# Two attention layers and two routed FFNs on one core: the bodies of the first FFN ahead of those of the second

## The reference

```python
x = x + attention0(layernorm(x), ctx, ctx)        # 32 query heads, 8 key heads of 8, no mask
x = x + ffn0(layernorm(x))                        # 2 experts, the better one per row
x = x + attention1(layernorm(x), ctx, Wq, Wkv, Wout)   # 16 heads of 16, causal
x = x + ffn1(layernorm(x))                        # 8 experts, two per row, and a shared one

# ffn0: h = n @ w_fc[e].T (256 -> 1024); a = square(where(h >= 0, h, h / 2)); a @ w_proj[e].T
# ffn1: h = n @ down_w + down_b (256 -> 128)
#       for the two experts of a row: gelu(gelu(h) @ w1 + b1) @ w2 + b2, by its gate
#       (the other experts get h = 0, whose result is the same for each row)
#       + 0.1 * the shared expert;  @ up_w + up_b;  + gelu(n) @ core_w + core_b
```

## Time and profile before

| | |
|---|---|
| median of 3 runs | 417.0 us (416.74 to 418.52) |
| the profiled execution | 420.97 us |
| its span, first to last instruction | 419.2 us |
| TensorE busy | 89% of the span |
| vector, scalar, GpSimd busy | 56%, 53%, 22% |
| mean granted TensorE clock | 0.935 of 2.4 GHz |
| DMA | busy in the first 3 of 40 slices |

### The profile page before, as it was taken

One profiled execution on the slowest core, in us unless ns is written; L12 is line 12 of the kernel. 1 busy time (PEld: TensorE's weight loads), 2 busy tenths in 40 slices (PEclk: granted clock), 3 DMA queues, 4 the chain that ended last, 5 costly groups with the idle time before them and its releaser, 6 DMA issues.

```text
span 419.2 us, 9361 instructions
## 1 busy us (share of the span) xinstructions
PE 373.0 (89%) x3768; PEld 302.9 (72%) x3768; DVE 235.2 (56%) x611; ACT 221.3 (53%) x419; POOL 93.3 (22%) x173
## 2 busy tenths in 40 slices
PE   3355939999999999997999999899998999996896
PEld 1343838888888877987778888588876888775574
DVE  4798494869587447788344212855348036436242
ACT  2344832654654555595684312667644236775662
POOL 7872112322123032310001334000053120002000
PEclk9975776999999999997999999699999999999699
DMA  9990000000000000000000000000000000000000
GB/s 190 410 396 11 2 0 2 2 2 2 2 2 0 3 2 2 2 2 0 2 3 27 2 0 1 2 1 2 14 16 1 2 0 2 3 2 25 0 2 26
DMA packets 8218, 12.16 MB, mean 29 GB/s; under 512 B 4464, under 2 KB 6768, under 8 KB 7408
## 3 DMA queue, kind: packets, MB, share of 16 engines
q1 hardware_dynamic: 8176, 11.57, 8.3%
HBM read 10.52 MB, written 1.05 MB: 28 GB/s over the span
## 4 chain that ended last, share of the span: by engine, by line
PE 73%; DVE 16%; ACT 5%; issue 3%; POOL 2%; POOLq 0%; DVEq 0%; ACTq 0%
PE Y L1226 23%; PE H L1226 22%; PE S L1226 15%; PE S L1267 4%; PE S L1327 3%; PE S L1291 1%; PE S L1234 1%; DVE PT L990 1%; DVE MN L989 1%; ACT A L778 1%; PE S L1243 1%; PE S L1392 1%; ACT L778 1%; DVE K L976 1%; DVE KT L1057 1%
## 5 line engine op out<-in xcount | busy, mean ns | idle before, releaser
L1226 PE MATMUL H<-XT,WF 128*128 128x256 f32 x256 | 62.5, 395 | 0.0
L869 POOL TENSOR_TENSOR A<-R 128x512 f32<-128x512 f32 x32 | 33.3, 1039 | 125.8 <-PE Y L1226 74.9
L1226 PE MATMUL Y<-WP,A 128*128 128x256 f32 x256 | 59.5, 382 | 0.0
L1226 PE MATMUL H<-GH,W 128*128 128x256 f32 x168 | 50.6, 407 | 7.1 <-ACT GH L769 4.2
L778 ACT ACTIVATE A<-H,B 128x256 f32<-128x256 f32 x84 | 38.9, 475 | 32.1 <-PE Y L1226 22.7
L1226 PEld LDWEIGHTS H<-XT,WF 128*128 128x128 f32 x256 | 49.0, 198 | 8.4 <-ACT R L752 0.8
L1226 PEld LDWEIGHTS Y<-WP,A 128*128 128x128 f32 x256 | 47.3, 190 | 6.1
L1226 PE MATMUL Y<-A,W 128*128 128x256 f32 x168 | 50.5, 397 | 0.2 <-ACT A L778 0.2
L752 ACT ACTIVATE R<-H 128x512 f32<-128x512 f32 x32 | 19.1, 597 | 46.2 <-PE H L1226 46.1
L1226 PEld LDWEIGHTS H<-GH,W 128*128 128x128 f32 x168 | 30.7, 199 | 14.4 <-ACT A L778 5.9
L1180 DVE TENSOR_TENSOR YG<-YS,Y 128x256 f32<-128x256 f32 x32 | 13.4, 420 | 39.1 <-ACT YS L795 39.0
(11 more groups left out here) (183 smaller groups left out, 647.1 us busy)
## 6 DMA issues: line engine op xcount, KB each, us to landing
W<-in_w SPq DMA_DIRECT2D x2, 1344.0 KB, 11.0
WF<-in_wf SPq DMA_DIRECT2D x2, 1024.0 KB, 7.8
WP<-in_wp SPq DMA_DIRECT2D x2, 1024.0 KB, 9.8
X<-in_x SPq DMA_DIRECT2D x8, 128.0 KB, 8.4
out_dram<-X SPq DMA_DIRECT2D x8, 128.0 KB, 1.7
CD<-in_ctx_in SPq DMA_DIRECT2D x2, 256.0 KB, 5.4
C<-in_ctx_in SPq DMA_DIRECT2D x1, 256.0 KB, 2.9
CT<-in_ctxT SPq DMA_DIRECT2D x1, 256.0 KB, 3.9
```

Of the source, the lines that this page charges most:

```text
L869: nc.gpsimd.tensor_tensor(flat(A0[:, n % 2, :, :]), R0[:, n % 2, :], R0[:, n % 2, :], ALU.mult).then_inc(a0_ready, 1)
L1226: return nc.tensor.matmul(o, a, b, start=start, stop=stop, skip_group_check=shared)
```

## The change

The order of bodies becomes all four of `ffn0`, then all four of `ffn1`. The numbers by which the planner weighs urgency, table loads, array changes and slack are others. Because the turned rows of one `ffn1` group may now be copied to XT1 soon after the GELU that reads those of the group before, this copy has a function of its own with a wait for that GELU (`gx_ready`).

```diff
-SWITCH = 5.3
-CHANGE = 8.0
-SLACK = {"pe": 0.039, "act": 0.052, "dve": 0.154, "pool": 0.024}
+SWITCH = 3.6
+CHANGE = 0.9
+SLACK = {"pe": 0.04, "act": 0.18, "dve": 0.31, "pool": 0.0}
...
-           "ffn0": (-33.7, 4.9), "ffn0_body": (-114.2, -4.5), "ffn1": (669.6, -114.4), "ffn1_body": (-36.9, 30.7),
+           "ffn0": (29.6, -29.4), "ffn0_body": (-151.7, -36.0), "ffn1": (617.6, -203.4),
...
-BODIES = [("ffn0", 0)] + [x for g in range(GROUPS - 1) for x in (("ffn0", g + 1), ("ffn1", g))] + [("ffn1", GROUPS - 1)]
+BODIES = [("ffn0", g) for g in range(GROUPS)] + [("ffn1", g) for g in range(GROUPS)]
...
-            h |= evacuate("ffn1", "x", lambda g, i: flat(XT1[:, :, :]), lambda b, i: b[:, :])
...
+            def turned_rows1(g, _):
+                b, done = filled(act, "ffn1", g, "x", 0)
+                if g:
+
+                    act.wait_ge(gx_ready, g)
+                nc.scalar.copy(flat(XT1[:, :, :]), b[:, :]).then_inc(done, 1)
```

More of the change, by code:

```diff
@@ L91 @@
 BODY = {("ffn0", "u"), ("ffn0", "d"), ("ffn0", "y"), ("ffn1", "c"), ("ffn1", "w"), ("ffn1", "y"), ("ffn1", "o")}
-URGENCY = {"attn0": (38.7, 20.0), "attn1": (-9.9, 32.6), "attn1_keys": (-23.0, -18.9),
-           "ffn0": (-33.7, 4.9), "ffn0_body": (-114.2, -4.5), "ffn1": (669.6, -114.4), "ffn1_body": (-36.9, 30.7),
-           "zero": (-347.7, 19.6), "constg": (-587.6, 61.3), "constm": (64.6, -29.8), "consti": (-58.3, 210.5)}
-BODIES = [("ffn0", 0)] + [x for g in range(GROUPS - 1) for x in (("ffn0", g + 1), ("ffn1", g))] + [("ffn1", GROUPS - 1)]
+URGENCY = {"attn0": (-3.3, -7.3), "attn1": (-12.5, 37.0), "attn1_keys": (-24.8, -58.7),
+           "ffn0": (29.6, -29.4), "ffn0_body": (-151.7, -36.0), "ffn1": (617.6, -203.4),
+           "ffn1_body": (-38.2, 30.7), "zero": (-524.0, 1.4), "constg": (-652.0, -20.7),
+           "constm": (-58.8, 97.7), "consti": (-191.2, 169.6)}
+BODIES = [("ffn0", g) for g in range(GROUPS)] + [("ffn1", g) for g in range(GROUPS)]
 def work_of(s):
@@ L799, in _ @@
                      ("ffn0", "g"): exps("ffn0", E0), ("ffn0", "u"): leaky, ("ffn1", "e"): exps("ffn1", E1),
-                     ("ffn1", "t"): top_exp, ("ffn1", "b"): gelu_biases, ("ffn1", "d"): inner,
+                     ("ffn1", "t"): top_exp, ("ffn1", "b"): gelu_biases, ("ffn1", "d"): inner, ("ffn1", "x"): turned_rows1,
                      ("ffn1", "c"): hidden, ("ffn1", "y"): expert})
```

## The result

The changed kernel takes 405.5 us, the median of 4 runs (402.2 to 407.1), against 417.1 before: ratio 0.9705, 95% interval 0.9636 to 0.9774. On another chip, with 6 runs, the ratio was 0.9728 (0.9698 to 0.9759). The forecast was 406.6. Its profiled execution took 407.12, span 405.2.

The account below looks back on a forecast made before the run. TensorE, busy 89% of the span, bounds the kernel; winnable time lies in the start and five stretches (20.6 us). Terms -5.0 - 4.3 - 3.7 - 1.2 - 1.4 - 1.3 + 4.5 + 2.0 = -10.4 from 417.0 give 406.6, range 399 to 418.

Parts of the forecast that it names:

- The start, -5: Before the first FFN's first up-projection: XN near 54.5, first H at 60 to 61 us, 5 us earlier; bounds 0 and -8.
- Group 0: Second FFN's first group: zero rows no longer among query turns; 0.5 of 4.8 us left, term -4.3.
- the border of bodies 0 to 1: Second FFN, group 1: 1.0 of 4.7 us left, term -3.7; sign: under 1.5 us idle.
- the border of bodies 1 to 2: Second FFN, group 2: gates ready early, two table loads; 1.0 of 2.2 us left, term -1.2; sign: under 1.5 idle.
- End of the attention: Stretch 368-382 us before, now under bodies 1 and 2: 0.8 of 2.2 us left, term -1.4.
- Last group: Second FFN, group 3: two table loads, not four, one gap of 3.1 us; 5.4 of 6.7 left, term -1.3.
- New places to wait, +2: From 60 to 230 us, attention fills the first FFN's bodies in an untraced order: +2 us, bounds 0 and 6.
- Array changes, +4.5: TensorE changes between tiled and whole array, 83 to 111, 0.16 us each: +4.5; sign: busy minus idle about 4 us longer.
- Table loads: Scalar engine: sixteen table loads, a switch costing 1.28 us; with the skill page's drain 2.66, result near 409.4.
- The added wait, 0: Copy of turned rows for groups 1 to 3 waits for the previous group's GELU: 0, at most 0.1 us a group.
- The slower one: Rival: second FFN bodies in a row each pay 8.9 us at their border; +19.3, 425.9 us; chance 0.13.
- The one in which the clock holds: Rival: no clock fall in the last lead-in (2.3) and no new waits (2.0); -14.7, 402.3 us; chance 0.15.

Follow-up runs that it names:

- old start, changed order behind: Changed kernel with every engine's list up to the first FFN's second down-projection as in the kernel before; 410.7 us, ratio 0.9815.
- changed, again: The changed kernel run again, unchanged, in a second series on another chip; 407.2 us, ratio 0.9728.
- late gates: Changed kernel with the last group's gates' turn behind two hidden chunks on TensorE, its copy behind the first hidden GELU; 404.3 us, ratio 0.9678.
- three moves: Changed kernel with the gates' turns of groups 0 and 3 and the turn of tile 6's attention result moved later; 401.8 us, ratio 0.9625.
- The moves: Changed kernel with five steps later on TensorE: gates' turns (groups 0, 3), query turns (tiles 6, 7), attention result's turn (tile 6); 406.1 us, ratio 0.9708.
- the three parts made alone: Kernel before with only the new start, 417.5 us, or only new SWITCH, CHANGE and SLACK, 439.1; changed kernel with all old planner numbers, 431.7.

## Why the prediction was right, and where it was not

The sum was right to 1.1 us (-11.6 measured, -10.4 forecast). Most of its steps stand, but that it came so close is in part luck. Between the two profiles, from which the terms were counted, the difference is 13.85; the profile of before was 4.0 above its median, that of the changed kernel 1.6. And terms that were too small and too large cancel.

*The start, -5.* H at 60.81, within the 60 to 61, and XN at 55.57, 1 us behind the 54.5. By my own formula the term is larger, 34.9 - 27.1 = 7.8 in the two profiles, and of another kind. I took H's earlier place as the gain and the half clock only as a bound (-8). In the first 80 us, TensorE's idle time fell by little and the clock's cost by much:

| first 80 us | idle | clock |
|---|---|---|
| before | 28.9 | 13.2 |
| old start, changed order behind | 29.1 | 11.5 |
| changed | 27.1 | 6.5 |
| changed, again | 28.1 | 7.1 |
| late gates | 27.8 | 8.6 |
| three moves | 27.6 | 5.6 |

So the start gives 1 to 2 us of idle time and 3 to 8 of clock. The reason given, that what now stands behind H is hidden because TensorE is never empty from there, is true only of the changed order: with the old one the same start gained nothing.

*Groups of the second FFN.* Group 0: no wait on its zero rows and none from 240 to 264 us. But its gates' turn waits 1.20 at 236, which I had not priced, and in five of seven traces with this wait a half clock follows (1.6 in this one). So 2.8 instead of 0.5 in this trace. Left at the border of bodies 0 to 1: 2.7 us instead of 1.0, three waits for keys and queries of tiles 6 and 7 (0.68, 0.79, 1.24), not for GX. This fails the sign "under 1.5 us idle". That term was too small because I counted the TensorE time of these steps, 6 us, as cover, and not that their turns wait for vector and GpSimd work. The moves also showed that those of the queries can't simply be put off. At the border of bodies 1 to 2: 0.9, as forecast. End of the attention: 0.3 instead of 0.8. Last group: 3.25 idle in one gap and 1.3 of clock, 4.5 instead of 5.4.

*New places to wait, +2.* In the stretch that I named, 60 to 230 us, TensorE is idle for only 0.4, at clock 1.00: the term was too large. What no term held is a half clock at 274 us, 1.7, with no gap ahead of it (see the last section).

*Array changes, +4.5.* 0.163 measured by itself, for one pair of shapes, against 0.16 read from two rows: 28 of them would be 4.6. In the kernel the work at full clock rose by only 2.4, in the second trace by 1.6; the sign "about 4 us longer" did not come. So the price holds for the change itself, and whether all 28 are paid in full in the kernel stays open.

*Table loads.* Sixteen. A switch costs 1.28 again: the load at 373.28 ends at 374.56, GX starts at 374.58. By the Trainium skill, "ScalarE: Activation LUTs", "What ACT_TABLE_LOAD costs", a drain of 1.38 would stand in between; it is not seen in this trace either.

*The added wait, 0*, as seen above.

With measured sizes, in the profiles: -7.8 for the start, 13.7 - 20.6 = -6.9 behind 80 us, +4.6: -10.1 against -13.85. The split of the span says where the 3.8 are. Idle and clock fell by 16.4, 1.7 more than these stretches hold: 1.0 of it is small waits of the kernel before outside my five stretches, the rest clock ahead of 59 us. And work at full clock rose by 2.4, 2.2 less than the changes would cost; that part stays open.

*The rivals.* The slower one (four bodies in a row each pay at their border) is not this kernel's case, but it was near: the same order of bodies under the old numbers takes 431.7, above its 425.9. I had priced the finished order and not the numbers that led to it; that was sound for this kernel, and says nothing of its neighbours. The one in which the clock holds, 402.3, is met in its number by the fastest run, which has the highest mean clock of the four. No trace of that run shows where it held:

| changed kernel, run | us | mean granted clock |
|---|---|---|
| fastest | 402.19 | 0.974 |
| | 404.49 | 0.966 |
| | 406.46 | 0.962 |
| profiled | 407.12 | 0.962 |

## What to carry to other kernels

Price a new plan from its finished order, stretch by stretch, and not part by part: here the three parts made alone cost 0, 15 and 22 us and all together gained 11.6. An earlier start of the bottleneck's main work gained nothing here where the steps behind it were not ready, and its worth is read from idle time and clock, not from where its first row stands. Once a plan is made, look for steps that its engine waits for and move them by hand behind one block of ready work, but only where no other engine is late behind them; a gap costs its length, and in some executions a half clock behind it.

## What was not expected of the hardware

Half clock came behind a stretch without any gap. In the changed kernel TensorE is idle for 0.1 of the 10 us from 264 to 274, with tiled blocks and zero-row products of one column, and then four records that take 1.03 at full clock take 1.91:

```profile
270.66 2.34 PE L1233 MATMUL S<-GB,W 128*128 128x1 f32 x20
...
274.96 1.91 PE L1233 MATMUL Y<-A,W 128*128 128x256 f32 x4
```

The kernel with three moves has the same at 269 us, after 39 us with 0.1 of idle time. In the second trace of the changed kernel the four records behind these rows take 1.03. Of nine traces with these rows five have this half clock. So neither the order nor the gaps alone settle where half clock falls; which executions get it, no run here explains.

The granted clock in the records does not always tell how fast TensorE ran. The old start in two kernels, the profile of before (granted 0.50 from 27 to 45 us) and the kernel with the old start in front of the changed order (granted 1.00), first before:

```profile
27.00:45.00 18.00, 12.30 (x128) 0.50 0.26 109
```

```profile
27.96 1.03 PE L1234 MATMUL S<-identb,QS 128*128 128x128 bf16 x8 [0.33 <-DVE PT L990]
29.28 1.11 PE L1267 MATMUL S<-identf,PT 128*128 128x128 f32 x4 [0.29 <-DVE PT L990]
```

and the other:

```profile
27.00:45.00 18.00, 12.35 (x130) 1.00 0.24 102
```

```profile
27.97 1.04 PE L1257 MATMUL S<-identb,QS 128*128 128x128 bf16 x8 [0.29 <-DVE PT L1013]
29.29 1.11 PE L1290 MATMUL S<-identf,PT 128*128 128x128 f32 x4 [0.29 <-DVE PT L1013]
```

Eight turns of QS take 1.03 and 1.04, where they take 0.62 at full clock (51.76 us in the changed kernel). So the duration of a row decides, not the column. The column showed nothing here for 18 us, and the split of the span would be wrong by some 6 us for that kernel, which is why it isn't in the table of the split. The Trainium skill, "TensorE: Matmul & The Clock Gate", "Seeing it yourself", warns that clock events in traces have been "observed to be unreliable"; these rows agree.
